# Product with the values: one burst of sixteen matmuls, or four pieces by key block spread over a group's slots

## The chip, the cores and the metric

One core of one Trainium2 chip runs the whole kernel. The metric is the device time of one execution in microseconds (us). Three executions of the kernel before took 763.6, 761.05 and 763.6 us; their median is 763.6 us.

## What is computed

Four sequences of 512 tokens with 128 channels (float32) go through two transformer layers with pre-normalisation and residuals. The change touches the two attention stages, each of 16 heads of width 8; in the second layer all heads share one key and one value head, and rotary tables are applied to queries and keys.

```python
x = x + L0_attn(layernorm(x), Wqkv, Wout)        # 16 heads, causal
x = x + L0_ffn(layernorm(x), ...)                # 8 experts, the best 2 weighted
x = x + L1_attn(layernorm(x), Wq, bq, ...)       # 16 query heads, 1 key and value head, rotary
x = x + L1_ffn(layernorm(x), ...)                # linear layers on values rounded to FP4 in blocks of 16

attn = einsum('nhqd,nhkd->nhqk', q, k) * scale   # then the causal mask, and a softmax over the keys
out  = einsum('nhqk,nhkd->nhqd', softmax(attn), v) @ Wout
```

## The kernel before, in words

All of the network is one launch. `network_order` (L187) writes one list of steps, and each engine walks the same list in that order and does its own part of each step (`attention_tensor`, L426, for TensorE; `attention_scalar`, L541, for ScalarE; `attention_vector`, L610, for VectorE; `attention_gpsimd`, L698; `attention_sync`, L388, for the DMA queue). An engine therefore never passes a step on which it waits. Semaphores carry the order between engines.

**Groups and steps.** A sequence's 16 heads are worked in four groups of four heads. `attention_order` (L75) makes a step s for each sequence, plus two to drain. Within step s and group g, two passes of different sequences are interleaved:

- `S` (L429) is the first pass, for sequence s: scores with the query on the partitions, in 11 units, 0 to 10. Units 0 to 2 and 7 to 10 fill 512 columns of a PSUM bank and units 3 to 6 fill 384. Each unit is one or more matmuls (L444) and one that adds the mask (L447). VectorE reduces each unit to row maxima (L663). There are two banks (`S_BANK`), so TensorE's unit n waits until unit n-2 has been reduced (L438).
- `ST` (L449) is the second pass, for sequence s-1: the scores again, with the key on the partitions, with the maxima (loaded through DRAM as three more rows) subtracted inside the matmul. There are five units (L465, masks L468, L469 or L473). ScalarE takes the exponential of each into `pT` (L557).
- `PV` (L476) multiplies the exponentials with the values of the group before: 4 key blocks times 4 heads, float32, each head in its own strip of 32 columns of the array (L486). Key block kb covers the queries from kb on: 512, 384, 256 and 128 columns. All of them accumulate in one bank (`O_BANK`), and ScalarE copies that bank to `oT` (L598).

**Slots.** A group has six slots, v = 0 to 5. Slot v holds S unit 2v, ST unit v, S unit 2v+1, and then the small steps that the table `misc` (L90) gives it (slot 5 has S unit 10 and table steps alone). These small steps are:

- `MP`: VectorE splits the negated maxima of the group before in three bfloat16 terms (L674 to L677).
- `MT`: TensorE turns these (L494; four matmuls with 12 columns of weights), ScalarE copies the result to `mrow` (L564), and the DMA queue stores it.
- `OT`: TensorE turns `oT` back (L524), and VectorE divides by the softmax sum (L685, L686).
- `XT`, `Q`, `K`, `V`, `QS`, `KS`: the normalised input is turned and projected for the next sequence. `ONT`, `WO`: the output projection of the sequence before the last.
- `VA`: GpSimd spreads the values of the next sequence into `vA` (L733, or L735 in the second layer, there after it has added a bias, L731). It waits until PV has read the old ones (L727).

**One bank for all small steps.** MT, OT, XT, Q, K, V, ONT and WO write the same PSUM bank, `misc`. `take` (L345) guards it: each of these steps first waits, on TensorE, for the semaphore by which the *previous* user of the bank was copied out, and then leaves its own. After MT that semaphore is `negm`, raised by ScalarE's copy L564:

```python
pe.wait_ge(a["mpart"], i + 1)      # MT, L491
take(a["negm"], i + 1)             # L492
pe.wait_ge(a["oTs"], i + 1)        # OT, L521
take(a["on"], i + 1)               # L522
```

Step 0 has only first-pass work, and steps 1 to 3 have both passes. Step 4 (`B`) has only the second pass and PV, merged with the routing of the next stage (first layer) or with the start of the last stage (second layer). Step 5 ends the attention.

Of the kernel before, what the change touches and what calls it, by code (L numbers as in the profile page):

```python
# [38 lines left out]
P = 128  # L39
B, T, D = 4, 512, 128  # L40
NB = T // P
NT = B * NB
H, DK = 16, 8
HG = 4
G = H // HG
VW = 32
# [15 lines left out]
O_BANK = 6  # L62
# [7 lines left out]
KB_AT = {0: (0, 512), 1: (512, 384), 3: (896, 128), 2: (1024, 256)}  # L70
PW = 1280
NV = HG + 1


def attention_order(layer):  # L75

    first = [("LN", 0, 0, 0), ("NORM", 0, 0, 0), ("XT", 0, 0, 0), ("Q", 0, 0, 0)]
    first += [("QS", 0, 0, 0), ("QH", 0, 0, 0)] * layer + [("K", 0, 0, 0), ("QM", 0, 0, 0)]
    first += [("KS", 0, 0, 0), ("KH", 0, 0, 0)] * layer + [("KM", 0, 0, 0), ("SPLITQ", 0, 0, 0), ("SPLITK", 0, 0, 0)]
    first += [("V", 0, 0, 0), ("LN", 1, 0, 0), ("NORM", 1, 0, 0)] + [("LOADA", 0, g, 0) for g in range(2)]
    steps = []
    for s in range(B + 2):
        o = []
        for g in range(G):
            turned = [("QS", s + 1, 0), ("QH", s + 1, 0)] * layer, [("KS", s + 1, 0), ("KH", s + 1, 0)] * layer
            misc = {  # L90
                0: [[("MP", s - 1, 3)], [("MT", s - 1, 3), ("PV", s - 2, 3), ("VA", s - 1, 0)], [("XT", s + 1, 0)],
                    [("OT", s - 2, 3)], [("Q", s + 1, 0)], turned[0]],
                1: [[("MP", s, 0)], [("MT", s, 0), ("PV", s - 1, 0)], [("K", s + 1, 0), ("QM", s + 1, 0)], [("ONT", s - 2, 0)],
                    turned[1], [("OT", s - 1, 0), ("KM", s + 1, 0)]],
                2: [[("MP", s, 1)], [("MT", s, 1), ("PV", s - 1, 1), ("SPLITQ", s + 1, 0), ("SPLITK", s + 1, 0)], [("WO", s - 2, 0)], [("LN", s + 2, 0)],
                    [("OT", s - 1, 1)], []],
                3: [[("MP", s, 2)], [("MT", s, 2), ("PV", s - 1, 2)], [("V", s + 1, 0)], [("NORM", s + 2, 0)],
                    [("OT", s - 1, 2)], []],
            }[g]
            for v in range(NV + 1):  # L100
                if s < B:
                    o.append(("S", s, g, 2 * v))
                if v < NV and 1 <= s <= B:
                    o.append(("ST", s - 1, g, v))
                if v < NV and s < B:
                    o.append(("S", s, g, 2 * v + 1))
                o += [(n, b, k, 0) for n, b, k in misc[v] if 0 <= b < B]

            ahead = [("LOADA", s + (g + 2) // G, (g + 2) % G), ("LOADB", s - 1 + (g + 2) // G, (g + 2) % G)]
            if s == 0:  # L110
                ahead = ahead[:1] + [("LOADB", 0, g - 2)] * (g >= 2)
            o += [(n, b, k, 0) for n, b, k in ahead if b < B]
        steps.append(o)
    return first, steps
# [117 lines left out]
def network(nc, z, wqkv, wout, cent, wp, bp, w1, b1, w2, b2, wq, bq, wk, bk, wv, bv, wo, bo,  # L232
            wg, wu, wd, rope_q, rope_k, pick, out):
    ctx = ExitStack()
    with ctx:
# [6 lines left out]
        ps = ctx.enter_context(nc.psum_tensor("ps", [P, 8, 512], F32))  # L242
# [44 lines left out]
        pT = sb("pT", [P, 2, HG, PW])  # L287
        vraw = sb("vraw", [P, 2, NB, D])
        vA = sb("vA", [P, NB, H, VW])
# [69 lines left out]
        made = sem("made")  # L359
# [18 lines left out]
        for layer in range(2):  # L378
            a = {n: sem(f"{n}_{layer}") for n in both + rotary * layer}
# [46 lines left out]
        def attention_tensor(pe, take, layer, name, b, g, u):  # L426
            a = A[layer]
            i = b * G + g
            if name == "S":  # L429
# [9 lines left out]
                w = (qb + 1) * P  # L439
# [34 lines left out]
                                         mask_kq[:].unsqueeze(1).broadcast_to([P, 2, P]), start=False, stop=True)  # L474
                last.then_inc(a["st"], 1)
            elif name == "PV":  # L476
                pe.wait_ge(a["ex"], (i + 1) * NV)
                if i == 0 and layer == 0:
                    pe.wait_ge(made, MADE)
                pe.wait_ge(a["va"], b + 1)  # L480
                if i:
                    pe.wait_ge(a["oTs"], i)
                for kb in range(NB):
                    off, w = KB_AT[kb]
                    for j in range(HG):
                        last = pe.matmul(ps[VW * j:VW * (j + 1), O_BANK, kb * P:T],  # L486
                                         vA[:, kb, g * HG + j if layer == 0 else 0, :],
                                         pT[:, g % 2, j, off:off + w], start=(kb == 0), stop=(kb == NB - 1))
                last.then_inc(a["pv"], 1)
            elif name == "MT":  # L490
                pe.wait_ge(a["mpart"], i + 1)  # L491
                take(a["negm"], i + 1)  # L492
                for qb in range(NB):
                    last = pe.matmul(misc[0:3 * HG, qb * P:(qb + 1) * P],  # L494
                                     mpart[:, g % 2, qb].rearrange("p k j -> p (k j)"), identb[:], start=True, stop=True)
                last.then_inc(a["mt"], 1)
            elif name == "XT":
                pe.wait_ge(N["norm"], 2 * B * layer + b + 1)
                take(a["xnT"], b + 1)
                for t in range(NB):  # L500
                    last = pe.transpose(misc[:, t * P:(t + 1) * P], xn[:, t, :], ident[:])
                last.then_inc(N["xt"], 1)
            elif name in ("Q", "QS", "K", "KS"):
                if b == 0 and layer == 0:
                    pe.wait_ge(made_w, 3)
                pe.wait_ge(a["xnT"], b + 1)
                done = {"Q": ("qrest", "qf")[layer], "K": ("krest", "kf")[layer], "QS": "rotq", "KS": "rotk"}[name]
                take(a[done], b + 1)
                w = {("Q", 0): wqp[0], ("Q", 1): wqp[1], ("QS", 1): wqs, ("K", 0): wkp, ("K", 1): wkr,
                     ("KS", 1): wks}[name, layer]  # L510
                m = w.shape[1]
                pe.matmul(misc[0:m, :], w[:], xnT[:], start=True, stop=True).then_inc(a[name.lower()], 1)  # L512
            elif name == "V":
                take(a["vraw"], b + 1)
                w = wqkv_sb[:, 2 * D:3 * D] if layer == 0 else wkv1[:, 1, :]
                m = D if layer == 0 else DK
                for t in range(NB):
                    last = pe.matmul(misc[:, t * m:(t + 1) * m], xnT[:, t * P:(t + 1) * P], w, start=True, stop=True)
                last.then_inc(a["v"], 1)
            elif name == "OT":  # L520
                pe.wait_ge(a["oTs"], i + 1)  # L521
                take(a["on"], i + 1)  # L522
                for t in range(NB):
                    last = pe.transpose(misc[:, t * P:(t + 1) * P], oT[:, t * P:(t + 1) * P], ident[:])  # L524
                last.then_inc(a["ot"], 1)
            elif name == "ONT":
                pe.wait_ge(a["on"], (b + 1) * G)
                take(a["onTs"], b + 1)
                for t in range(NB):
                    last = pe.transpose(misc[:, t * P:(t + 1) * P], on[:, t, :], ident[:])  # L530
                last.then_inc(a["ont"], 1)
            elif name == "WO":
                pe.wait_ge(a["onTs"], b + 1)
                take(a["xdone"], b + 1)
                for t in range(NB):
                    last = pe.matmul(misc[:, t * P:(t + 1) * P], onT[:, t * P:(t + 1) * P], wo_sb[layer][:],
                                     start=True, stop=True)
                last.then_inc(a["wo"], 1)


        def attention_scalar(act, layer, name, b, g, u):  # L541
            a = A[layer]
# [42 lines left out]
            elif name in ("QM", "KM"):  # L585
                c, m = "QK".index(name[0]), (P, SR)[layer and name == "KM"]
                act.wait_ge(a[name[0].lower() + "rest"], b + 1)
                act.activation(part[0:m, c, 1, :], rest_of(layer, c)[0:m], ACT.Copy).then_inc(a[name[0].lower() + "mid"], 1)
            elif name == "V" and layer == 0:
                act.wait_ge(a["v"], b + 1)  # L590
                if b >= 2:
                    act.wait_ge(a["va"], b - 1)
                act.activation(vraw[:, b % 2].rearrange("p n d -> p (n d)"), misc[:], ACT.Copy).then_inc(a["vraw"], 1)
            elif name == "PV":
                act.wait_ge(a["pv"], i + 1)
                if i:
                    act.wait_ge(a["ot"], i)
                act.activation(oT[:], ps[:, O_BANK, :], ACT.Copy).then_inc(a["oTs"], 1)  # L598
            elif name == "ONT":
                act.wait_ge(a["ont"], b + 1)  # L600
                if b:
                    act.wait_ge(a["wo"], b)
                act.activation(onT[:], misc[:], ACT.Copy).then_inc(a["onTs"], 1)
# [846 lines left out]
```

## Time and profile before

| | |
|---|---|
| Times of three executions | 763.6, 761.05, 763.6 us |
| Span of the profiled execution, first to last instruction | 757.7 us |
| Instructions | 13009 |
| TensorE busy, matmul / weight load | 660.7 us (87%) / 464.5 us (61%) |
| VectorE busy | 514.1 us (68%) |
| ScalarE busy | 342.2 us (45%) |
| GpSimd busy | 151.8 us (20%) |
| PV matmuls (L486) | 1024 records, 77.9 us of TensorE's time |
| Row maxima (L663) | 352 reductions, 215.5 us of VectorE's time |

The profiled execution's time is told as its span; the median of the runs is 5.9 us above it, for what lies before the first and after the last instruction. In the rows, PE is TensorE's matmul side and PEld its weight loads, DVE is VectorE, ACT is ScalarE, POOL is GpSimd. Successive matmuls overlap: a matmul's row starts before the row ahead of it has ended, so a busy row is not a full array. A float32 matmul leaves two records.

### The profile page before, as it was taken

The page shows a single profiled execution, that of the slowest core. Times are in us where ns is not written, and L with a number is a line of the kernel's source. Part 1 is how long each engine was busy: PE and PEld are TensorE (multiplying, and loading weights), DVE is VectorE, ACT ScalarE, POOL GpSimd, SP SyncE. Part 2 cuts the span into 40 slices and gives each one's busy share as a digit, 9 for nine tenths or more (in the row PEclk, how much of TensorE's full clock was granted, in tenths as well). Part 3 has the DMA queues.
Part 4 walks back from the last instruction along what each step waited for, and adds up shares of the span by engine and source line. Part 5 has one row for each costly group of instructions (what it writes and reads, how often), then busy time and mean ns, then how long its engine had stood idle before and what let it go on. Part 6 is the DMA issues. An engine that isn't in the chain of part 4 may idle for free.

```text
span 757.7 us, 13009 instructions
## 1 busy us (share of the span) xinstructions
PE 660.7 (87%) x5007; PEld 464.5 (61%) x5007; DVE 514.1 (68%) x1313; ACT 342.2 (45%) x472; POOL 151.8 (20%) x145
## 2 busy tenths in 40 slices
PE   1478889999989899999999998999989899998664
PEld 0333556565655699898998785775555655555443
DVE  6578776777743536658537467777786778666993
ACT  1110566656575444433444432335546455674221
POOL 5301010100011010010021301302203010345764
PEclk9995999999999999999999999999999999999985
DMA  5405876454320000000000200211211211000000
GB/s 152 126 22 147 173 218 132 85 141 75 66 55 14 1 1 1 1 1 1 1 1 1 63 1 12 75 23 28 83 42 27 65 45 35 25 12 1 14 15 28
DMA packets 29325, 38.07 MB, mean 50 GB/s; under 512 B 3719, under 2 KB 23185, under 8 KB 29265
## 3 DMA queue, kind: packets, MB, share of 16 engines
q1 hardware_dynamic: 29265, 37.25, 20.3%
q8 instruction: 40, 0.66, 0.4%
q14 instruction: 20, 0.16, 0.1%
HBM read 26.33 MB, written 10.88 MB: 49 GB/s over the span
## 4 chain that ended last, share of the span: by engine, by line
PE 64%; DVE 25%; issue 5%; ACT 3%; POOL 1%; DMA 0%; POOLq 0%; DVEq 0%; ACTq 0%
PE ps L989 14%; PE ps L486 9%; PE ps L444 7%; DVE mx L663 6%; PE ps L465 6%; PE ps L979 4%; PE ps L512 3%; PE ps L981 3%; PE ps L980 3%; DVE xn L926 3%; PE ps L447 2%; ACT pT L557 1%; PE ps L494 1%; PE ps L469 1%; DVE x L1063 1%
## 5 line engine op out<-in xcount | busy, mean ns | idle before, releaser
L663 DVE TENSOR_REDUCE mx<-ps 128x1 f32<-128x384 f32 (+3 forms) x352 | 215.5, 637 | 72.5 <-PE ps L447 70.4
L557 ACT ACTIVATE pT<-ps 128x1024 f32<-128x1024 f32 x160 | 162.1, 1023 | 86.9 <-PE ps L469 71.9
L1024 ACT ACTIVATE pT<-ps,b1c 128x512 f32<-128x512 f32 x128 | 87.8, 687 | 129.6 <-PE ps L981 128.7
L989 PEld LDWEIGHTS ps<-w_sb,pT 128*128 128x128 f32 x1024 | 132.2, 191 | 11.8 <-issue 1.3
L989 PE MATMUL ps<-w_sb,pT 128*128 128x128 f32 x1024 | 135.5, 275 | 0.0
L447 PE MATMUL ps<-mask_qk,identb 128*128 128x128 bf16 (+2 forms) x352 | 90.2, 256 | 0.0
L444 PE MATMUL ps<-stA 96*128 96x128 bf16 (+3 forms) x256 | 69.6, 332 | 19.2 <-DVE mx L663 14.3
L486 PE MATMUL ps<-pT,vA 128*32 128x512 f32 (+3 forms) x1024 | 77.9, 439 | 0.7 <-ACT pT L557 0.7
L1063 DVE SCALAR_TENSOR_TENSOR x<-ps,comb,x 128x128 f32<-128x128 f32 x128 | 36.0, 344 | 58.4 <-PE ps L989 58.3
L444 PE MATMUL ps<-kA,stA 96*128 96x128 bf16 (+3 forms) x256 | 63.7, 304 | 12.8 <-DVE mx L663 11.6
L979 PE MATMUL ps<-x_hi,w_hi 128*128 128x512 f32 x128 | 62.9, 491 | 1.2 <-DVE w_lo L1045 1.0
L486 PEld LDWEIGHTS ps<-pT,vA 128*32 128x32 f32 x1024 | 40.0, 110 | 32.3 <-issue 22.0
L444 PEld LDWEIGHTS ps<-stA 96*128 96x128 bf16 x256 | 21.6, 101 | 49.9 <-DVE mx L663 35.5
L981 PE MATMUL ps<-x_hi,w_lo 128*128 128x512 f32 x128 | 50.5, 395 | 0.0
L980 PE MATMUL ps<-x_lo,w_hi 128*128 128x512 f32 x128 | 50.4, 394 | 0.0
L465 PE MATMUL ps<-stB 96*128 96x512 bf16 (+3 forms) x256 | 48.4, 301 | 0.9 <-ACT pT L557 0.5
L465 PE MATMUL ps<-stB,kA 96*128 96x512 bf16 (+3 forms) x256 | 48.4, 301 | 0.6 <-ACT pT L557 0.4
L444 PEld LDWEIGHTS ps<-kA,stA 96*128 96x128 bf16 x256 | 21.7, 98 | 36.3 <-DVE mx L663 24.7
L447 PEld LDWEIGHTS ps<-mask_qk,identb 128*128 128x128 bf16 x352 | 35.9, 102 | 6.4 <-issue 3.7
L598 ACT ACTIVATE oT<-ps 128x512 f32<-128x512 f32 x32 | 19.1, 597 | 44.4 <-PE ps L486 44.4
L926 DVE TENSOR_SCALAR xn<-x,mv,rstd 128x128 f32<-128x128 f32 x64 | 30.3, 687 | 8.9 <-POOL rstd L933 8.9
L469 PE MATMUL ps<-mask_kq,identb 128*128 128x256 bf16 x128 | 34.8, 272 | 0.0
(232 smaller groups left out, 964.1 us busy)
## 6 DMA issues: line engine op xcount, KB each, us to landing
stA<-stack_scratch SPq DMA_DIRECT2D x48, 192.0 KB, 3.4
stB<-stack_scratch SPq DMA_DIRECT2D x48, 192.0 KB, 4.5
stack_scratch<-part SPq DMA_DIRECT2D x12, 384.0 KB, 3.2
w_sb<-in_L_ffn_W_dram SPq DMA_DIRECT2D x16, 256.0 KB, 5.6
stack_scratch<-part SPq DMA_DIRECT2D x12, 256.0 KB, 3.1
stack_scratch<-part SPq DMA_DIRECT2D x12, 128.0 KB, 3.1
x<-in_L_attn_z_dram SPq DMA_DIRECT2D x4, 256.0 KB, 4.4
out_dram<-x SPq DMA_DIRECT2D x4, 256.0 KB, 2.3
```

The lines of the kernel that those rows point to most:

```text
L444: pe.matmul(ps[:, bank, m * w:(m + 1) * w], stA[:, 0, h, qb * P:w], kk[:, 0:w], start=(m == 0), stop=False)
L447: pe.matmul(diagonal, identb[:], mask_qk[:].unsqueeze(1).broadcast_to([P, len(heads), P]), start=False, stop=True).then_inc(a["sc"], 1)
L465: pe.matmul(o, kk[:, kb * P:(kb + 1) * P], stB[:, 0, h, kb * P:T], start=(at % 512 == 0), stop=False)
L486: last = pe.matmul(ps[VW * j:VW * (j + 1), O_BANK, kb * P:T], vA[:, kb, g * HG + j if layer == 0 else 0, :], pT[:, g % 2, j, off:off + w], ...
L557: act.activation(dst_, src, ACT.Exp, scale=SCALE).then_inc(a["ex"], 1)
L663: nc.vector.tensor_reduce(mx[:, g % 2, qb, heads[0]:heads[0] + nh], ps[:, S_BANK[n % 2], 0:nh * w].rearrange("p (h k) -> p h k", h=nh), AX ...
L926: ins = nc.vector.tensor_scalar(xn[:, t, :], xs[:, t, :], mv[:, t, 0:1], rstd[:, t:t + 1], ALU.subtract, ALU.mult)
L979: pe.matmul(bank, w_hi[:, slot, fs], x_hi[:, b % 2, :], start=True, stop=False)
L980: pe.matmul(bank, w_hi[:, slot, fs], x_lo[:, b % 2, :], start=False, stop=False)
L981: pe.matmul(bank, w_lo[:, slot, fs], x_hi[:, b % 2, :], start=False, stop=True).then_inc(M["h"], 1)
L989: last = pe.matmul(ps[:, ST_BANK[1] + m % 2, f * P:(f + 1) * P], hT[:, (m % 2) * FC + c, f * P:(f + 1) * P], w2_sb[:, e, c, :], start=(c = ...
L1024: act.activation(hT[:, (m % 2) * FC + f, :], ps[:, ST_BANK[0] + n % 2, :], ACT.Gelu, bias=b1c[:, e * FC + f:e * FC + f + 1]).then_inc(M["g ...
```

## The change

PV becomes four pieces, one for each key block. Piece u is issued by TensorE in slot u+1 (slots 1 to 4), right behind the second S unit and ahead of the slot's table steps. Before, all four were issued in slot 1, behind MT. The waits of PV stand at piece 0 alone, and its semaphore is raised by piece 3; ScalarE's copy of the bank (L598) moves with piece 3 to slot 4. OT of a group moves from slots 3 to 5 of the group in which its PV runs (OT of a sequence's last group, in slot 3; of the first, in slot 5; of the others, in slot 4) to slot 1 of the group after, directly behind MT.

```diff
             misc = {
-                0: [[("MP", s - 1, 3)], [("MT", s - 1, 3), ("PV", s - 2, 3), ("VA", s - 1, 0)], [("XT", s + 1, 0)],
-                    [("OT", s - 2, 3)], [("Q", s + 1, 0)], turned[0]],
-                1: [[("MP", s, 0)], [("MT", s, 0), ("PV", s - 1, 0)], [("K", s + 1, 0), ("QM", s + 1, 0)], [("ONT", s - 2, 0)],
-                    turned[1], [("OT", s - 1, 0), ("KM", s + 1, 0)]],
-                2: [[("MP", s, 1)], [("MT", s, 1), ("PV", s - 1, 1), ("SPLITQ", s + 1, 0), ("SPLITK", s + 1, 0)], [("WO", s - 2, 0)], [("LN", s + 2, 0)],
-                    [("OT", s - 1, 1)], []],
-                3: [[("MP", s, 2)], [("MT", s, 2), ("PV", s - 1, 2)], [("V", s + 1, 0)], [("NORM", s + 2, 0)],
-                    [("OT", s - 1, 2)], []],
+                0: [[("MP", s - 1, 3)], [("MT", s - 1, 3), ("VA", s - 1, 0), ("OT", s - 2, 2)], [("XT", s + 1, 0)],
+                    [], [("Q", s + 1, 0)], turned[0]],
+                1: [[("MP", s, 0)], [("MT", s, 0), ("OT", s - 2, 3)], [("K", s + 1, 0), ("QM", s + 1, 0)], [("ONT", s - 2, 0)],
+                    turned[1], [("KM", s + 1, 0)]],
+                2: [[("MP", s, 1)], [("MT", s, 1), ("OT", s - 1, 0), ("SPLITQ", s + 1, 0), ("SPLITK", s + 1, 0)],
+                    [("WO", s - 2, 0)], [("LN", s + 2, 0)], [], []],
+                3: [[("MP", s, 2)], [("MT", s, 2), ("OT", s - 1, 1)], [("V", s + 1, 0)], [("NORM", s + 2, 0)], [], []],
             }[g]
...
+                if 1 <= v <= NB and 0 <= p[0] < B:
+                    o.append(("PV", p[0], p[1], v - 1))
                 o += [(n, b, k, 0) for n, b, k in misc[v] if 0 <= b < B]
...
             elif name == "PV":
-                pe.wait_ge(a["ex"], (i + 1) * NV)
...
-                for kb in range(NB):
-                    off, w = KB_AT[kb]
-                    for j in range(HG):
...
-                last.then_inc(a["pv"], 1)
+                if u == 0:
+                    pe.wait_ge(a["ex"], (i + 1) * NV)
...
+                off, w = KB_AT[u]
+                for j in range(HG):
+                    last = pe.matmul(ps[VW * j:VW * (j + 1), O_BANK, u * P:T],
+                                     vA[:, u, g * HG + j if layer == 0 else 0, :],
+                                     pT[:, g % 2, j, off:off + w], start=(u == 0), stop=(u == NB - 1))
+                if u == NB - 1:
+                    last.then_inc(a["pv"], 1)
...
-            elif name == "PV":
+            elif name == "PV" and u == NB - 1:
                 act.wait_ge(a["pv"], i + 1)
```

Here `p` is the group before: (s-1, g-1), or (s-2, 3) for g = 0.

## Rows read from the trace of the kernel before

**Rows 1.** The page: busy time by engine, and the chain that ended last.

```profile
PE 660.7 (87%) x5007; PEld 464.5 (61%) x5007; DVE 514.1 (68%) x1313; ACT 342.2 (45%) x472; POOL 151.8 (20%) x145
...
PE 64%; DVE 25%; issue 5%; ACT 3%; POOL 1%; DMA 0%; POOLq 0%; DVEq 0%; ACTq 0%
```

**Rows 2.** Waits, 130 to 215 us: waiter, releaser: us in total, times, longest.

```profile
DVE mx L663 <- PE ps L447: 18.0, 24, 1.9
...
PE ps L530 <- DVE q L619: 0.5, 1, 0.5
```

**Rows 3.** Stretches: length, busy us (x instructions) PE, PEld, DVE, ACT, POOL, clock, DMA.

```profile
149.87:161.04 11.17, 10.71 (x107) 7.01 (x107) 8.20 (x19) 6.17 (x8) 0.00 (x0) 1.00 0.79 209
161.04:171.93 10.89, 10.57 (x107) 6.98 (x108) 7.62 (x18) 6.79 (x9) 0.00 (x0) 1.00 0.42 78
595.06:608.82 13.76, 12.15 (x108) 7.85 (x109) 9.61 (x22) 6.16 (x8) 0.00 (x0) 0.88 0.13 32
```

**Rows 4.** Timeline, DVE, 161.6 to 173 us: start, us, instruction, [idle before].

```profile
163.72 0.56 DVE L663 TENSOR_REDUCE mx<-ps 128x1 f32<-128x384 f32 x1 [1.89 <-PE ps L447]
...
168.93 2.00 DVE L663 TENSOR_REDUCE mx<-ps 128x1 f32<-128x512 f32 x3
170.85 0.17 DVE L674 TENSOR_SCALAR mpart<-mx 128x16 bf16<-128x16 f32 x1
...
171.47 0.18 DVE L677 TENSOR_TENSOR mpart<-mrest,mpart 128x16 bf16<-128x16 f32 x1
```

**Rows 5.** Timeline, PE, 163 to 172 us, the same group: start, us, instruction.

```profile
163.29 0.34 PE L444 MATMUL ps<-stA 96*128 96x384 bf16 x1
...
163.53 0.60 PE L465 MATMUL ps<-stB 96*128 96x512 bf16 x3
...
164.13 0.33 PE L444 MATMUL ps<-stA 96*128 96x384 bf16 x1
164.35 1.11 PE L518 MATMUL ps<-wqkv_sb,xnT 128*128 128x128 f32 x8
165.30 0.33 PE L444 MATMUL ps<-stA 96*128 96x384 bf16 x1
...
168.08 0.38 PE L444 MATMUL ps<-stA 96*128 96x512 bf16 x1
...
168.67 0.38 PE L444 MATMUL ps<-stA 96*128 96x128 bf16 x4 [0.15 <-DVE mx L663]
...
169.11 0.60 PE L465 MATMUL ps<-stB 96*128 96x512 bf16 x3
...
169.72 0.38 PE L444 MATMUL ps<-stA 96*128 96x256 bf16 x2
...
170.27 0.39 PE L444 MATMUL ps<-stA 96*128 96x256 bf16 x2
...
170.61 0.60 PE L465 MATMUL ps<-stB 96*128 96x512 bf16 x3
...
171.21 0.33 PE L444 MATMUL ps<-stA 96*128 96x384 bf16 x1
...
171.71 0.33 PE L494 MATMUL ps<-identb,mpart 128*12 128x128 bf16 x3
```

**Rows 6.** Timeline, PE, 218 to 223 us: a PV without MT ahead of it.

```profile
219.34 0.27 PE L469 MATMUL ps<-mask_kq,identb 128*128 128x256 bf16 x1
219.54 2.36 PE L486 MATMUL ps<-pT,vA 128*32 128x512 f32 x32
221.83 1.12 PE L946 MATMUL ps<-q,wp_sb 128*128 128x512 f32 x2
```

**Rows 7.** ScalarE's copy L564: instances, ns min/median/max, first and last start.

```profile
L564 ACT ACTIVATE mrow<-ps x32: 569/570/587, 51.6 to 653.2; 12x512 bf16<-12x512 f32 x32
```

**Rows 8.** GpSimd's bias and its spreading of the values in the second layer.

```profile
L731 POOL TENSOR_TENSOR x<-x,bob x4: 1267/1270/1277, 489.8 to 656.8; 128x512 f32<-128x512 f32 x4
L735 POOL COPY vA<-vraw x4: 210/212/213, 491.1 to 658.0; 128x32 f32<-128x32 f32 x4
```

More of the change, by code:

```diff
@@ L89, in attention_order @@
             turned = [("QS", s + 1, 0), ("QH", s + 1, 0)] * layer, [("KS", s + 1, 0), ("KH", s + 1, 0)] * layer
+            p = (s - 1, g - 1) if g else (s - 2, G - 1)
             misc = {
-                0: [[("MP", s - 1, 3)], [("MT", s - 1, 3), ("PV", s - 2, 3), ("VA", s - 1, 0)], [("XT", s + 1, 0)],
-                    [("OT", s - 2, 3)], [("Q", s + 1, 0)], turned[0]],
-                1: [[("MP", s, 0)], [("MT", s, 0), ("PV", s - 1, 0)], [("K", s + 1, 0), ("QM", s + 1, 0)], [("ONT", s - 2, 0)],
-                    turned[1], [("OT", s - 1, 0), ("KM", s + 1, 0)]],
-                2: [[("MP", s, 1)], [("MT", s, 1), ("PV", s - 1, 1), ("SPLITQ", s + 1, 0), ("SPLITK", s + 1, 0)], [("WO", s - 2, 0)], [("LN", s + 2, 0)],
-                    [("OT", s - 1, 1)], []],
-                3: [[("MP", s, 2)], [("MT", s, 2), ("PV", s - 1, 2)], [("V", s + 1, 0)], [("NORM", s + 2, 0)],
-                    [("OT", s - 1, 2)], []],
+                0: [[("MP", s - 1, 3)], [("MT", s - 1, 3), ("VA", s - 1, 0), ("OT", s - 2, 2)], [("XT", s + 1, 0)],
[5 more added lines that the diff above has]
+                3: [[("MP", s, 2)], [("MT", s, 2), ("OT", s - 1, 1)], [("V", s + 1, 0)], [("NORM", s + 2, 0)], [], []],
             }[g]
@@ L476, in attention_tensor @@
             elif name == "PV":
-                pe.wait_ge(a["ex"], (i + 1) * NV)
[L478 to L482, printed above, removed]
-                for kb in range(NB):
-                    off, w = KB_AT[kb]
-                    for j in range(HG):
-                        last = pe.matmul(ps[VW * j:VW * (j + 1), O_BANK, kb * P:T],
-                                         vA[:, kb, g * HG + j if layer == 0 else 0, :],
-                                         pT[:, g % 2, j, off:off + w], start=(kb == 0), stop=(kb == NB - 1))
-                last.then_inc(a["pv"], 1)
+                if u == 0:
+                    pe.wait_ge(a["ex"], (i + 1) * NV)
+                    if i == 0 and layer == 0:
+                        pe.wait_ge(made, MADE)
+                    pe.wait_ge(a["va"], b + 1)
+                    if i:
+                        pe.wait_ge(a["oTs"], i)
+                off, w = KB_AT[u]
[5 more added lines that the diff above has]
+                    last.then_inc(a["pv"], 1)
             elif name == "MT":
```

## The prediction

> **What bounds the kernel now.** I read the page first: it gives TensorE's matmul side 87% of the span and 64% of the chain that ended last, VectorE 68% and 25% [rows 1]. The waits of a stretch of first-layer attention come next: VectorE's reductions sat idle for TensorE for 18.0 us in 85, the longest time 1.9 us [rows 2]. The timeline places that longest one: the reduction at 163.72 waited 1.89 us, while TensorE worked off MT and the burst of PV [rows 4]. The change aims at this hole. Then I cut the stretch into groups, from burst to burst: 11.17 and 10.89 us in the first layer, of which matmuls fill 10.71 and 10.57 and VectorE only 8.20 and 7.62; one group of the second layer takes 13.76, with VectorE at 9.61 [rows 3]. So a group is paced by TensorE's list, not by VectorE, and filling VectorE's hole gains only what TensorE itself waits for.
>
> How much that is shows in start-to-start distances [rows 5]. A 384-column S unit with nothing in its way takes 0.22 us (164.13 to 164.35), an ST unit 0.60 (163.53 to 164.13), V 0.95 (164.35 to 165.30). Where TensorE waits, the distance is longer: S unit 10 to unit 0 takes 0.59 (168.08 to 168.67) where a 512-column unit needs 0.28, so 0.31 lost; unit 1 to unit 2 takes 0.55 (169.72 to 170.27) where unit 2 to ST takes 0.34 (170.27 to 170.61), so 0.21 lost; unit 3 to MT takes 0.50 (171.21 to 171.71) where 0.22 would do, so 0.28 lost. Sum 0.80 of 10.89 us. No more can be gained in this group.
>
> **The change, part by part.**
>
> *PV itself* has the same matmuls. A PV with no MT ahead of it takes 2.29 us from its start to that of the next matmul [rows 6]. Less 0.09 for the switch behind it (next part) this is 2.20 for 1280 columns: 0.88, 0.66, 0.44 and 0.22 us for the four pieces. Net cost nothing.
>
> *Switches between strips of 32 columns and the whole array.* Between matmuls on the whole array the next starts 0.16 us before the end of the last: V's last record ends at 164.35 + 1.11 = 165.46, and the next S starts at 165.30 [rows 5]. Into PV it is 0.07 (219.34 + 0.27 = 219.61 against 219.54), and out of it 0.07 (221.90 against 221.83) [rows 6]. Each switch thus costs 0.09 us. Before there are two in a group, now eight: six more are 0.56 us. The Trainium skill, "TensorEngine Tiling (Array Packing)", Key Properties, says that changing the tiling mode drains TensorE, and gives no price; by that rule, which speaks against this change, the trace agrees, at 0.09 us.
>
> *OT behind MT.* This is the wait that the change adds. OT has to `take` the shared bank, so TensorE waits until ScalarE has copied MT out (L564, 0.57 us [rows 7]). Before, the burst of PV stood between MT and the bank's next user and covered this. Now nothing does, and S unit 4 and ST unit 2 queue behind OT on TensorE; VectorE's OT, and the reduction of unit 4 behind it, wait as well. MT's last matmul ends about 0.38 us after its first starts (the first three make one row of 0.33 [rows 5], the fourth 0.05 later, an estimate). Then 0.04 us for a semaphore (estimate), 0.57 copy, and 0.04 again: OT starts 1.03 after MT, where TensorE is free 0.22 after. The wait is 0.81 us, and hides the switch out of piece 0. Bounds: at least the copy less nothing, 0.57; at most 0.81 plus some 0.5, if ScalarE is still at the exponential of ST unit 1. ScalarE isn't by this walk: that exponential starts two steps earlier, and S unit 3 and piece 0 (0.22 + 0.09 + 0.88 = 1.19) pass before MT. I take 0.81.
>
> *What goes.* The 0.28 before MT: piece 0 (0.88 us) now covers VectorE's four small operations, 170.85 to 171.65 [rows 4]. They hid the switch of 0.09 into PV and MT, which piece 0 now pays in the open; that one is within the eight counted. The 0.21 before unit 2 goes too, as VectorE no longer has OT between units 9 and 10 (three reductions in 2.00 us follow it [rows 4]). The 0.31 before unit 0 stays: by my walk unit 8 starts at 0, unit 9 at 0.94, its reduction ends at 2.11, piece 3 ends at 1.62 and unit 10 at 1.90, so unit 0 waits until 2.2. Sum of this kind of group (with V): +0.56 + 0.81 − 0.28 − 0.21 = +0.9 us.
>
> *The other three kinds*, walked alike. With WO: 11.17 against 10.89 us on an equal list, so 0.28 more of waits [rows 3]; VectorE's addition now comes between slack slots, and I let them go: +0.6. With K and ONT: ONT's wait for K (0.5 [rows 2]) goes, as a slot and a piece lie between: +0.4. With Q: VectorE's subtraction holds unit 10 and TensorE as before, so only MT's 0.28 goes: +1.1. Mean 0.75. Each layer has 11 groups with S and PV (step 1 from group 1, steps 2 and 3): 22 × 0.75 = +16.5 us.
>
> *Groups without S* (step 4, and the last PV): five a layer, with six more switches, 10 × 0.56 = 5.6; they share TensorE with other stages' steps and wait partly for ScalarE, so half: +2.8. *Groups that VectorE paces* (second layer, such as the 13.76 us one [rows 3]), three of the 22: extra TensorE time lies beside VectorE's: −2.3.
>
> *Costed at nothing.* ScalarE's copy of the PV bank moves behind the last exponential; TensorE has slots 5 and 0 and half of slot 1 before it needs the bank, and ScalarE is busy 6.8 of 10.9 us [rows 3]. If that cover failed, piece 0 would wait for 0.6 us of copy. GpSimd's VA starts after piece 3 and not after slot 1: it takes 1.27 + 0.21 us in the second layer [rows 8], and about 2.9 us pass before the next group's piece 0. No DMA issue is moved; MT's store comes some 0.8 us later and is read a step later.
>
> Sum: 16.5 + 2.8 − 2.3 = +17.0. The rows' execution spans 757.7 us, 5.9 below the median of the runs, 763.6; I add to the median: **780.6 us**.
>
> **Rivals.**
>
> *Faster, through VectorE's hole.* If the reductions are what really paces a group, the loss is their idle 1.89 us [rows 4]. They would now wait only for OT, some 1.1 us; 0.7 to 0.8 come back in each of 22 groups, 16 us: 748 us. For it: the chain gives VectorE 25% [rows 1], and TensorE's rows overlap, so that 87% overstates it. It decides if the three waits (0.80) shrink by more than the new wait and the switches (1.37) cost; the distances say that they can't. Chance 0.10. The Trainium skill, "Trainium Kernel Development and Optimization", Performance Expectations, says to judge TensorE by its weight loads' busy share, not its matmuls'; weight loads fill 61% [rows 1], and by that rule there is room and this rival is right. The trace is against it inside a group: the distances of neighbouring matmuls add up to nearly all of the time though weight loads fill 6.98 of 10.89 us [rows 3].
>
> *Not slower: switches and OT fall into waits.* If the six switches lie where TensorE waits for a reduction anyway, and ScalarE copies sooner, 0.6 of OT's wait stands against 0.5 to 0.8 of waits that go: 22 × 0.1 = +2, about 766 us. For it: TensorE waits in most slots of the second layer. Against: slots 2 and 3 show no wait now, and OT's is in series. Chance 0.16.
>
> *Much slower: the values are late.* If GpSimd starts VA late behind its other work, TensorE stands at piece 0 of group 1, with S and ST behind it, by 1 to 2 us, three times a layer, and the Q groups lose more than I walked: +8, about 789 us. It decides when VA ends over 2.9 us after piece 3. Chance 0.12.
>
> The forecast has 0.62. The order of steps is written out, so the pieces do go where they are said to go; I give nothing to the change not taking place.
>
> **How the numbers follow.** About 0.5% is what a measurement of this kernel can tell from no change. Low end: the second rival with OT's wait at 0.57 lies at 762 to 766; the first rival and part of a tail stay out. High end: 22 × 0.5 for ScalarE being late at OT gives 792. Range 762 to 791. Faster by over 0.5%: the first rival and a sliver of the second, 0.11. Within 0.5% (759.8 to 767.4): most of the second, 0.14. Slower: 0.75.
>
> **What would show it.** In the changed profile, TensorE's matmul or weight load of L524's successor waits for ScalarE's copy of `mrow` some 22 times, about 0.8 us each; the hole of 1.9 us before unit 4's reduction is replaced by one of about 1.1 that OT's matmuls end; MT no longer waits for `mpart`; weight loads next to PV pieces show idle "issue" 32 × 8 times; a group with V takes 11.8 us against 10.89. I am wrong if OT doesn't wait, if groups get shorter, or if GpSimd or ScalarE's bank copy appears as what PV waits for.

## The result and the profile after

The changed kernel takes 793.6 us (median of four runs, 792.15 to 796.02) against 762.33 for the kernel before, a ratio of 1.0424 with a 95% interval of 1.0388 to 1.0460. The forecast was 780.6 us with a range of 762 to 791: the direction was right, the size was half of the true one, and the value lies above the range. The profiled execution spans 792.1 us against 757.7.

The page of the changed kernel, its engines and two of its groups (columns as in the front table: busy time and its share; then busy us, mean ns of one, idle time before and its releaser):

```profile
PE 685.7 (87%) x5007; PEld 452.9 (57%) x5007; DVE 519.1 (66%) x1313; ACT 342.9 (43%) x472; POOL 150.7 (19%) x145
...
L489 PE MATMUL ps<-pT,vA 128*32 128x512 f32 (+3 forms) x1024 | 97.0, 453 | 1.5 <-ACT oT L602 1.3
...
L528 PE MATMUL ps<-ident,oT 128*128 128x128 f32 x128 | 20.4, 282 | 20.7 <-ACT mrow L568 20.0
```

As many instructions ran as before. PV's rows fill 97.0 us of TensorE's time where they filled 77.9. Rows overlap their neighbours, so that difference is not time lost: what a PV costs is read from start-to-start distances below. OT now waits 20.0 us for ScalarE's copy of MT, which ended no wait of OT in the kernel before. In the waits of the whole run this is:

```profile
PE ps L528 <- ACT mrow L568: 20.0, 21, 2.4
```

So the added wait occurs 21 times, mostly at 0.8 us, with the longest at 2.4. The kind of group that the prediction walked, a group with V, shows it in the timeline of TensorE (start, us, instruction, [idle before]):

```profile
165.87 0.22 PE L450 MATMUL ps<-mask_qk,identb 128*128 128x128 bf16 x1
166.02 1.06 PE L489 MATMUL ps<-pT,vA 128*32 128x512 f32 x8
166.90 0.39 PE L498 MATMUL ps<-identb,mpart 128*12 128x128 bf16 x4
168.06 0.63 PE L528 MATMUL ps<-ident,oT 128*128 128x128 f32 x4 [0.77 <-ACT mrow L568]
168.52 0.33 PE L447 MATMUL ps<-stA 96*128 96x384 bf16 x1
...
169.66 0.85 PE L489 MATMUL ps<-pT,vA 128*32 128x384 f32 x8
170.45 1.16 PE L522 MATMUL ps<-wqkv_sb,xnT 128*128 128x128 f32 x8
171.44 0.33 PE L447 MATMUL ps<-stA 96*128 96x384 bf16 x1
...
172.64 0.64 PE L489 MATMUL ps<-pT,vA 128*32 128x256 f32 x8
173.21 0.39 PE L447 MATMUL ps<-stA 96*128 96x512 bf16 x1
...
174.53 0.43 PE L489 MATMUL ps<-pT,vA 128*32 128x128 f32 x8
174.88 0.39 PE L447 MATMUL ps<-stA 96*128 96x512 bf16 x1
...
178.19 0.64 PE L489 MATMUL ps<-pT,vA 128*32 128x512 f32 x4
```

From piece 0 to the next piece 0 are 12.17 us (166.02 to 178.19), where the same group took 10.89 [rows 3] and the walk gave 11.8. MT starts straight behind piece 0, so its wait for the maxima is gone, as forecast. OT starts 1.16 us after MT, where 1.03 was forecast. Each change between PV's strips and the whole array shows an overlap of 0.07 us rather than 0.16, as in [rows 6]; MT, which stands right behind piece 0, overlaps it by 0.18, so nothing is paid there. VectorE's hole of 1.89 us [rows 4] has become two, one for OT and one of 1.53 us behind piece 1 and V:

```profile
168.72 0.26 DVE L689 RECIPROCAL rec<-ps 128x16 f32<-128x16 f32 x1 [1.38 <-PE ps L528]
...
171.87 0.56 DVE L667 TENSOR_REDUCE mx<-ps 128x1 f32<-128x384 f32 x1 [1.53 <-PE ps L450]
```

Split by the 32 MTs as marks, the 34.4 us lie as follows: from the first to the 16th MT (first layer, up to step 4) 172.2 us against 161.3; from there to the first MT of the second layer 257.8 against 251.9; in the second layer 199.7 against 188.1; from the last MT to the end 111.1 against 105.1. These stretches need two corrections. In the changed kernel piece 0 stands ahead of MT, so that each layer's marks take in one piece 0 (0.88 us) that they did not take in before. And 1.7 us arose in step 0, where both kernels do the same work (31.8 us against 30.1 from the first to the fourth MT, and 30.1 to 31.8 in the other runs); they are not of the change. So the growth divides as follows (forecast for the groups: 11 × 0.75 in each layer, less 2.3 in the second):

| Part of the run | grew by, us | forecast |
|---|---|---|
| first layer, 11 groups with both passes | 8.6 | 8.25 |
| second layer, 11 groups with both passes | 10.9 | 5.95 |
| steps 4 and 5 of both layers, and what they are merged with | 13.2 | 2.8 |
| step 0, not of the change | 1.7 | 0 |

### The profile page after: what moved, and what is told of

Same layout as the page of the kernel before. It is cut to its first block, busy times and chain, and to the rows that moved or that the text cites. A ratio compares the mean times of both kernels' runs of the same rounds, so it can differ in the third digit from the quotient of the medians.

```text
span 792.1 us, 13009 instructions
## 1 busy us (share of the span) xinstructions
PE 685.7 (87%) x5007; PEld 452.9 (57%) x5007; DVE 519.1 (66%) x1313; ACT 342.9 (43%) x472; POOL 150.7 (19%) x145
## 4 chain that ended last, share of the span: by engine, by line
PE 68%; DVE 21%; ACT 4%; issue 4%; POOL 2%; DMA 0%; POOLq 0%; DVEq 0%; ACTq 0%
PE ps L993 13%; PE ps L489 9%; PE ps L447 8%; PE ps L468 8%; DVE mx L667 5%; PE ps L983 4%; PE ps L985 3%; PE ps L516 3%; PE ps L984 3%; DVE xn L930 3%; PE ps L450 3%; PE ps L528 2%; PE ps L472 1%; ACT mrow L568 1%; PE ps L540 1%
## 5 line engine op out<-in xcount | busy, mean ns | idle before, releaser
L667 DVE TENSOR_REDUCE mx<-ps 128x1 f32<-128x384 f32 (+3 forms) x352 | 217.9, 638 | 50.2 <-PE ps L450 47.7
L489 PE MATMUL ps<-pT,vA 128*32 128x512 f32 (+3 forms) x1024 | 97.0, 453 | 1.5 <-ACT oT L602 1.3
L489 PEld LDWEIGHTS ps<-pT,vA 128*32 128x32 f32 x1024 | 20.6, 108 | 31.3 <-issue 29.1
L528 PE MATMUL ps<-ident,oT 128*128 128x128 f32 x128 | 20.4, 282 | 20.7 <-ACT mrow L568 20.0
L689 DVE RECIPROCAL rec<-ps 128x16 f32<-128x16 f32 x32 | 8.2, 256 | 43.6 <-PE ps L528 43.6
```

Of the source, the lines that this page charges most:

```text
L489: last = pe.matmul(ps[VW * j:VW * (j + 1), O_BANK, u * P:T], vA[:, u, g * HG + j if layer == 0 else 0, :], pT[:, g % 2, j, off:off + w], s ...
L667: nc.vector.tensor_reduce(mx[:, g % 2, qb, heads[0]:heads[0] + nh], ps[:, S_BANK[n % 2], 0:nh * w].rearrange("p (h k) -> p h k", h=nh), AX ...
```

## The experiments

All ratios are to the kernel before, from runs on the same chip, with 95% intervals. The edits are shown shortened. Theory A was the prediction's: OT's wait behind MT is the largest term, the switches the second.

### MT ahead of piece 0

```diff
-  [("MT", s, 1), ("OT", s - 1, 0), ...]      # and PV piece 0 ahead of the table
+  MT, then PV piece 0, then [("OT", s - 1, 0), ...]
```

> MT goes ahead of piece 0, so that piece 0 (0.88 us) stands between MT and OT. Theory A (OT's wait for ScalarE's copy of MT is the largest term): the wait before OT falls from 0.93 us to about 0.1 in the 21 groups, and a wait of about 0.4 for VectorE's split of the maxima comes back before MT; 22 x 0.45 = 10 us less than the changed kernel, some 783 us. Theory B (spreading the pieces is what costs, and OT's wait takes time that VectorE needs anyway): no change, 792 to 795 us.

Measured: 785.8 us, 1.0322 (1.0274 to 1.0370). A group with V takes 11.65 us against 12.17: TensorE no longer waits at OT and waits 0.40 longer at MT. The direction and most of the size are theory A's. Three groups of the second layer still wait 1.1 to 1.6 us at OT, and by the marks all of the gain lies in the first layer: its 11 groups are 4.7 us shorter than in the changed kernel, those of the second layer are 0.5 longer.

### OT in slot 2

```diff
-  slot 1: MT, OT      slot 2: V
+  slot 1: MT          slot 2: OT, V     (likewise with XT, K, WO)
```

> OT goes to slot 2, behind piece 1, so that two S units, one ST unit and piece 1 (1.8 us) cover ScalarE's copy of MT. Theory A: TensorE loses 0.84 us less in each of 22 groups (0.93 less the switch of 0.09 that the wait hid), and the long waits of the second layer (2.56, 2.56, 1.47) shrink by 1.5 each: 18 + 3 = 21 us less, some 772 us. Theory B: TensorE's waits for reductions come back in slots 2 to 0, at most 5 us less, 788 us or more.

Measured: 784.5 us, 1.0311 (1.0274 to 1.0348): 9 us less, not 21. The timeline of its TensorE tells why:

```profile
168.74 0.66 PE L528 MATMUL ps<-ident,oT 128*128 128x128 f32 x4
170.08 1.16 PE L522 MATMUL ps<-wqkv_sb,xnT 128*128 128x128 f32 x8 [0.68 <-DVE on L690]
```

OT itself no longer waits, but V, the next user of the bank, now waits for VectorE to read OT out. The group with V takes 12.21 us, as before the edit; the one after it, which has nothing in slot 2 besides OT, takes 10.37 where it took 11.18. So it isn't ScalarE's copy alone that costs: *two users of the one bank in one slot* cost a wait also where VectorE is the reader between them. Theory A had named only the first pair.

### Fewer bursts: pieces 1 to 3 in slot 2, and two bursts in slots 1 and 4

```diff
-                if 1 <= v <= NB ...:  PV piece v - 1
+                if v in (1, 2) ...:   PV piece 0 in slot 1, pieces 1, 2, 3 in slot 2
```

> Piece 0 stays in slot 1, pieces 1 to 3 go together in slot 2: four switches of the tiling fewer in each of 32 PV, and PV ends one and a half slots earlier. By switches at 0.09 us: 32 x 0.37 = 12 us less, and 2 to 5 more because GpSimd's VA and what queues behind it come earlier: 776 to 780 us. If OT's wait alone matters: 790 us.

```diff
-                if 1 <= v <= NB ...:  PV piece v - 1
+                if v in (1, NB) ...:  PV pieces 0, 1 in slot 1, pieces 2, 3 in slot 4
```

> Pieces 0 and 1 in slot 1, pieces 2 and 3 in slot 4: also four switches fewer in each PV, but PV ends in slot 4 as in the changed kernel, so GpSimd's VA is as late. By switches: 12 us less, some 781 us, 2 to 5 us above the kernel with pieces 1 to 3 in slot 2. If switches are hidden in other waits: 790 us or more.

Measured: 795.8 us, 1.0469 (1.0423 to 1.0515) for the first and 786.4 us, 1.0322 (1.0262 to 1.0382) for the second. The first was a miss: four switches fewer bring nothing if the burst starves VectorE, which now sits idle for 2.19 us behind pieces 1 to 3 and V (1.53 in the changed kernel). The group with V is no shorter (12.16 us): TensorE waits 0.31 us for a reduction before S unit 10, where it didn't wait, and 0.44 before unit 0, where it waited 0.31; in other groups such waits reach 1.45. The second, with the same number of switches, has a group with V of 11.45 us, 0.72 less. Four switches are 0.37 of that, the seams between pieces (told below) and V's some 0.15, and the wait before unit 0 went (unit 10 to unit 0 takes 0.29 instead of 0.59), against 0.08 more before unit 2. Where a burst stands decides as much as how many there are.

### OT alone in slot 3

```diff
-  slot 1: MT, OT      slot 3: (ONT in group 1)
+  slot 1: MT          slot 3: OT          (ONT in slot 5 of group 1)
```

> OT alone in slot 3 behind piece 2 (ONT goes to slot 5 of its group), so that no two users of the shared bank stand in one slot. In the kernel with OT in slot 2 the wait only moved, from OT to V, WO, K or XT behind it. If it is the bank's round trip that costs (0.84 us in each of 22 groups, and 1.5 more in three), all of it goes here: a group with V falls from 12.17 to 11.3 us, and the whole by 18 to 21 us, to 772 to 776 us, leaving some 12 us above the kernel before for the switches. If OT's work on VectorE only moves the wait to a reduction: at most 8 us less, 785 us.

Measured: 772.9 us, 1.0159 (1.0126 to 1.0193): 20 us less than the changed kernel, as forecast from the corrected theory. Its group with V, with the columns of [rows 3]:

```profile
161.60:172.95 11.35, 11.21 (x105) 6.45 (x101) 7.95 (x19) 6.80 (x9) 0.00 (x0) 1.00 0.39 71
```

Where the remainder lies was not as expected. The 22 groups with both passes take only 0.9 us more than in the kernel before (122.0 against 121.6 in the first layer, 132.9 against 132.4 in the second): what the six switches cost there is won back by waits that went. (One of these groups ran at a mean granted clock of 0.86 and took 12.4 us, where the changed kernel's took 10.9.) So OT's place is 18.6 of the 19.5 us that these groups had lost. Nearly all that is left lies in steps 4 and 5 and what they are merged with, where the stretch from the 16th MT to the second layer is even longer than in the changed kernel (261.7 us against 257.8).

### OT behind MT in the kernel before

The reverse: PV stays whole, and only OT is moved.

```diff
-  slot 1: MT, PV      slots 3 to 5: OT of this PV
+  slot 1: MT, OT of the group before, PV
```

> The kernel before with one thing added: OT moves to slot 1 of the next group, between MT and the unbroken PV. It gets the wait for the shared bank (0.8 us in some 21 groups, 2.5 in two or three of the second layer) and one pair of switches more (its first is hidden in the wait, so 0.1), and nothing else of the change: 22 x 0.9 + 3 = 18 to 23 us more than the kernel before, 780 to 785 us. If the loss of the changed kernel came from the spreading alone: 763 us.

Measured: 815.1 us, 1.0738 (1.0706 to 1.0771): 55 us above the kernel before, far more than the 20 expected, and more than the whole change. In its timelines:

```profile
183.20 0.39 PE L494 MATMUL ps<-identb,mpart 128*12 128x128 bf16 x4 [0.24 <-DVE mpart L677]
184.40 0.63 PE L524 MATMUL ps<-ident,oT 128*128 128x128 f32 x4 [0.82 <-ACT mrow L564]
184.96 0.64 PE L486 MATMUL ps<-pT,vA 128*32 128x512 f32 x4
```

The wait at OT is the known one (0.82). But a group with V is 1.57 us longer, as the wait is not alone: VectorE stands still through MT, OT and PV, and TensorE later waits for it at S units 10 and 0 and at MT (0.24 here). In the waits of the whole run OT's are 22.9 us of the 55:

```profile
PE ps L524 <- ACT mrow L564: 22.9, 21, 2.4
```

By the marks the first layer's 11 groups are 16.3 us longer and the second's 27.1. The second layer also had a lower granted clock (columns of [rows 3]; this kernel first, then the kernel before):

```profile
540.00:700.00 160.00, 132.69 (x1073) 72.74 (x1071) 102.39 (x237) 74.55 (x90) 22.16 (x23) 0.91 0.14 37
```

```profile
510.00:652.00 142.00, 128.20 (x1134) 78.21 (x1131) 107.95 (x249) 79.07 (x96) 23.29 (x23) 0.99 0.18 45
```

A mean of 0.91 against 0.99: the record shows TensorE at the lower of its two levels (1.2 rather than 2.4 GHz) for 27 of the 160 us, in six stretches. Three of them adjoin the waits at OT of 2.0 to 2.4 us; the other three stand in groups whose wait at OT is 0.8 to 1.1. At half the speed 27 us cost at most 14 (an estimate from these rows), so the clock can't be all of the 27.1, and what part it has was not separated. So the wait's cost isn't additive. The run also shows that the split did bring something: with OT directly behind MT in both, four pieces (1.0424) are 24 us faster than one burst (1.0738).

### VA in slot 4, and steps 4 and 5

```diff
-  group 0, slot 1: VA
+  group 0, slot 4: VA
```

> Only GpSimd's VA moves, from slot 1 to slot 4 of group 0, where the last piece of PV now ends. If VA holds up what stands behind it on GpSimd (the normalisation of the next stage, for whose turning TensorE waited 2.76 us), that wait goes: 3 us less, up to 5 if the second layer has the like; 789 to 791 us. Otherwise 793 us as the changed kernel.

```diff
+                one = s >= B
-                if 1 <= v <= NB ...:  PV piece v - 1
+                if 1 <= v <= NB ...:  as before; pieces 1, 2, 3 in slot 2 where one
```

> From step 4 on, where there is no first pass, pieces 1 to 3 go together in slot 2; the rest is the changed kernel. Ten PV with two pairs of switches fewer: 10 x 0.45 = 4.5 us less, and VA is earlier by one and a half slots: 2 less. Expected 787 to 789 us if steps 4 and 5 lose by switches; 793 us if they lose by the shared bank and by how the list of the next stage falls between.

Measured: 790.5 us, 1.0393 (1.0367 to 1.0420), and 791.1 us, 1.0395 (1.0373 to 1.0418). Both take 2 to 3 us off; the intervals overlap that of the changed kernel, so the size rests on the timelines. TensorE of the changed kernel in step 4, then of the kernel with VA in slot 4:

```profile
232.47 0.81 PE L945 MATMUL ps<-ident,xn 128*128 128x128 f32 x4 [2.60 <-DVE xn L930]
```

```profile
227.22 0.66 PE L945 MATMUL ps<-ident,xn 128*128 128x128 f32 x4 [0.27 <-DVE xn L930]
```

GpSimd walks the list in order too. In the changed kernel VA waits there for the last piece of PV. Behind it stood the reciprocal square root of the next stage's normalisation, behind that VectorE's normalisation, and behind that the turning at L945, for which TensorE waited 2.60 us:

```profile
229.33 0.61 POOL L737 COPY vA<-vraw 128x512 f32<-128x512 f32 x1 [42.43 <-PE ps L489]
...
230.23 1.04 POOL L937 TENSOR_TENSOR rstd<-veps,half 128x4 f32<-128x4 f32 x1
```

The kernel with pieces 1 to 3 in slot 2 from step 4 on ends PV, and so VA, earlier as well: its wait at this turning is 0.64 us. So its 2 us are mostly the same ones, and the two runs' gains must not be added.

### The list's length

```diff
-                o += [(n, b, k, 0) for n, b, k in misc[v] if 0 <= b < B]
+                o += [(n, b, k, u) for n, b, k in misc[v] if 0 <= b < B for u in range(NB if n == "PV" else 1)]
```

> The kernel before, with PV entered in the list as four steps in a row in slot 1, as MT ahead of them: every engine does the same work in the same order within attention, but the attention's list is as long as in the changed kernel, so that where it is merged with another stage's list (step 1 of the first layer, steps 4 and 5 of both, step 0 of the second) the other stage's steps fall elsewhere. The changed kernel lost 5.9 us from its 16th group to the second layer and 6.0 us after the 32nd, and at most 5 of these 12 are told by VA and the switches. If the shift tells the rest: 4 to 6 us above the kernel before, 765 to 767 us. If not: within 0.3% of it.

Measured: 764.8 us, 1.0052 (1.0033 to 1.0072): 4 us for nothing but three more entries in the list for each PV. `merged` interleaves two lists by the fraction of each that is done, so longer attention lists put the steps of the experts' stage elsewhere. In its trace (span 4.0 us longer) all of it lies from the 16th MT to the second layer (256.9 us against 251.9); the second layer's groups are 1.4 us shorter, and the end is the same (105.3 against 105.1).

### Putting the parts together

Two bursts and OT in slot 3; then VA in slot 4 as well; then each burst as a single entry of the list; and, by itself, the kernel before with PV ahead of MT:

```diff
 # two bursts (slots 1 and 4), OT in slot 3
+  group 0, slot 4: VA
+  o.append(("PV", p[0], p[1], 0 if v == 1 else 2))   # a burst of two pieces is one entry
 # apart from these, in the kernel before:
-  slot 1: MT, PV
+  slot 1: PV, MT
```

> OT in slot 3 as in the run before, and PV in two bursts (pieces 0 and 1 in slot 1, 2 and 3 in slot 4). Against the kernel with four pieces and OT in slot 3 (1.016 of the kernel before) four switches fewer in each PV. In the changed kernel this took 0.72 us from a group with V; the same here gives 11.35 - 0.7 = 10.7 us for that group and 8 to 12 us in all: 761 to 765 us, the same as the kernel before. If waits for reductions return, 768 us.

> The same with GpSimd's VA in slot 4. In the changed kernel that took 3 us off; here 2 to 3 us: 758 to 762 us. All of the changed kernel's loss would then be told by its three parts: the shared bank, the switches, VA.

> The best of the split kernels (OT in slot 3, VA in slot 4, bursts in slots 1 and 4; 0.9973 of the kernel before), with each burst as one step of the list, so the list is two steps shorter for each PV. If the shift of merged lists costs, part of it comes back: 1 to 3 us less, 755 to 757 us. If not, 758 us.

> The kernel before with PV ahead of MT in slot 1, and nothing else: PV covers VectorE's split of the maxima, for which TensorE waited 0.27 us before MT, and the bank's next user comes two S units and an ST unit later (1.05 us), which just covers ScalarE's copy. 22 x (0.27 - 0.09) = 4 us less than the kernel before, and up to 2 more in the second layer, where the wait was 0.77 in two groups: 756 to 758 us against 762. If that copy is late, the next user of the bank waits 0.1 to 0.3 us, and nothing is gained: 761 to 764 us.

| Kernel | us | ratio to before |
|---|---|---|
| two bursts, OT in slot 3 | 760.5 | 1.0014 (0.9989 to 1.0039) |
| and VA in slot 4 | 757.7 | 0.9973 (0.9960 to 0.9986) |
| and a burst is one entry | 757.2 | 0.9939 (0.9916 to 0.9962) |
| kernel before, PV ahead of MT | 756.6 | 0.9945 (0.9928 to 0.9962) |

All four came out within 0.6 us of the range expected. From four pieces to two bursts is 1.0159 − 1.0014 or 11 us. In the traces the 22 groups with both passes are 10.2 us shorter, about what four switches and the seams come to (22 × (0.37 + 0.12) = 10.8). Outside them the stretch from the 16th MT to the second layer is 7.8 us shorter and the end 1.7 longer, which switches alone do not tell. VA is 0.0041 or 3 us. The last two beat the kernel before by about half a per cent, one by a split done with care, the other by exchanging two entries; they can't be told apart. Nor is the step from two entries of the list to one for a burst settled: the intervals of the ratios overlap, and in its trace the stretch from the 16th MT to the second layer is 2.7 us longer, not shorter, so a shorter list is not by itself a better one. The group with V of the kernel with two bursts and VA in slot 4:

```profile
160.90:171.50 10.60, 10.60 (x105) 6.67 (x101) 7.67 (x17) 6.89 (x8) 0.00 (x0) 1.00 0.51 91
```

Matmul rows cover all of its 10.60 us, 0.3 less than the kernel before (10.89 [rows 3]). Over the 22 groups with both passes this kernel gains 9.4 us (116.4 against 121.6 and 128.2 against 132.4), and loses most of it again elsewhere. So with its neighbours well placed the split does pay where both passes run. Two bursts there and the unbroken PV from step 4 on, which this points to, were not tried.

## Why the prediction was right and wrong

The forecast was +17.0 us on a median of 763.6; the profiled executions differ by 34.4, the medians of the runs by 31.3. (The 5.9 us between the profiled span and that median were put down to what lies before the first and after the last instruction. In each run that lists both, this is only 1.8 us; the rest is that the profiled execution was a quicker one. The forecast growth does not hang on it.) By the table above, the first layer's groups came out, in sum, as forecast. The steps that failed are the term for steps 4 and 5, 2.8 us where 13.2 were measured, and the second layer's groups, 5.95 where 10.9 were measured.

**What bounds the kernel: right.** TensorE's list paces a group. The Trainium skill ("Trainium Kernel Development and Optimization", Performance Expectations) says that weight loads' busy share (beside MFU, the share of peak that is used), and not the matmuls', tells how near a kernel is to its roofline. The prediction read it as room in the list, and that reading does not hold here: in the group above the matmul rows leave no gap with weight loads at 6.67 of 10.60 us, so 63% is not slack.

**The switches: right in price, short in what hangs on them.** 0.09 us each was seen at the edges of the pieces. But pieces have seams as well: from start to next start they take 0.88, 0.78, 0.57 and 0.36 us; less a switch (none behind piece 0), 0.88, 0.69, 0.48 and 0.27 against the forecast 0.88, 0.66, 0.44 and 0.22. That is +0.12 where the text said "net cost nothing". V right behind a piece takes 0.99 us (170.45 to 171.44) rather than 0.95.

**OT behind MT: the mechanism right, the size short.** From MT to OT passed 1.16 us, not 1.03. ScalarE's copy between them starts 0.43 us after MT and takes 0.59, as forecast to 0.03:

```profile
167.33 0.59 ACT L568 ACTIVATE mrow<-ps 12x512 bf16<-12x512 f32 x1 [0.40 <-PE ps L498]
```

But OT (168.06) starts 0.14 us after its end, where the text had estimated 0.04 without a row. And three groups of the second layer waited 2.4, 1.3 and 2.4 us, together 3.7 more than 0.8 each; this is most of what the second layer's groups fell short by. The timeline of all engines in one of the longest shows why:

```profile
549.64 0.63 ACT L592 ACTIVATE part<-q 48x512 bf16<-48x512 f32 x1 [1.26 <-POOL q L721]
549.91 0.20 PEld L498 LDWEIGHTS ps<-identb,mpart 128*12 128x12 bf16 x4 [0.92 <-DVE mpart L681]
549.91 0.39 PE L498 MATMUL ps<-identb,mpart 128*12 128x128 bf16 x4
550.18 1.91 ACT L561 ACTIVATE pT<-ps 128x1024 f32<-128x1024 f32 x2
550.35 1.15 POOL L726 TENSOR_TENSOR part<-q,part 48x512 bf16<-48x512 f32 x1 [0.74 <-ACT part L592]
551.99 0.57 ACT L568 ACTIVATE mrow<-ps 12x512 bf16<-12x512 f32 x1
```

ScalarE waits for GpSimd in KM, the last step of group 1 (L592), and two exponentials of group 2 stand behind it and before the copy, which starts 2.1 us after MT. The upper bound in the text (0.5 more, "if ScalarE is still at the exponential") was the right case for these groups, though 2.4 us lie well above even that bound; it was dropped on a walk of the first layer alone.

**What goes: nearly right.** MT's wait went; 0.07 of the 0.21 before S unit 2 stayed (176.51 to 176.93 in the full timeline is 0.42, where 0.34 would do). Together: the group with V grew by 1.28 us, 0.9 forecast; Q by 1.43 (1.1), WO by 0.98 (0.6), K by 0.69 (0.4). All four are 0.3 to 0.4 short. That the 11 groups of the first layer still sum to 8.6 us against 8.25 is luck: other groups, in step 1 above all, grew by less than the kind that they were counted as (one there is 0.65 us shorter). In the second layer the 2.3 us that were taken off for groups paced by VectorE did not show: the 13.76 us group fell by 0.4 only, and that with a mean granted clock of 0.88 before and 1.00 after, and the layer's groups lost more than the first's.

**"Costed at nothing": wrong for VA.** The text checked whether VA would be in time for PV, and it was. It did not ask who is queued behind VA on GpSimd: 2.60 us of TensorE's wait. The other item, ScalarE's later copy of the PV bank, ended one wait of PV in the whole run, 1.3 us in the first layer's last PV.

**Steps 4 and 5: 2.8 forecast, 13.2 measured; the step that failed most.** Half of the switches was a guess without rows. VA is 3 us; the run that removes part of the switches there took 2 off, but mostly by ending VA's wait too. The longer list costs 5.0 us in the first layer's share when nothing else changes, and was not thought of: the change adds three entries for each PV to lists that are merged by fraction. Whether these add up wasn't tried; behind the last MT even the two-burst kernel with VA moved takes 108.9 us against 105.1. So VA is shown as a cause, the list's length only in the kernel before, and how the rest of the 13.2 us divides stays open.

**The rivals.** The fast rival fell: the three waits of TensorE that filling VectorE's hole could gain were 0.80 us in the group with V, as the distances had said, and the new wait and the switches cost more. The late-values rival had VA right as a danger, but at PV, where GpSimd ended no wait. Of the signs named beforehand, OT's waits (21), the end of MT's wait and a longer group came. The hole ended by OT was 1.38 us instead of 1.1, and a second of 1.53 came that had not been foreseen.

## What to carry to other kernels

If several small steps share one bank, a cover between two of them is worth as much as the steps: before work is moved out of a list, ask which round trip it was hiding, and put no two users of a bank in one slot (here that was 18.6 of 19.5 us in the groups with both passes). A hole on an engine that doesn't pace the group is worth only what the pacing engine itself waits for (0.8 of 10.9 us here), and cheap edits may get at that directly. When a wait is added or moved, follow every queue that holds it, GpSimd's too, and where lists are merged by their length, look at the stages that they are merged with: here the loss in those stages was more than four times the forecast.

## What was not expected of the hardware

Moving OT behind MT in the kernel before cost 55 us, of which the waits at OT are 22.9. Three of them, in the second layer, were 2.0 to 2.4 us long, and the granted clock had a mean of 0.91 over 160 us there, against 0.99. TensorE's matmuls on 32-column strips overlap their neighbours on the whole array by 0.07 us rather than 0.16 in both directions: in the changed kernel's trace this is the median of 124 entries into PV and of 100 exits from it, and 0.16 the median of the other pairs of neighbouring rows.
